# Value matmuls of two attention units issued back to back, with three buffers of probabilities

## The reference

```python
mod = (_silu(L0_c) @ L0_wmod).reshape(L0_c.shape[0], 6, 1, -1)
sa, ca, ga, sb, cb, gb = (mod[:, 0], ..., mod[:, 5])      # ga, gb kept at least 0.25 from zero
h = _layernorm(x) * (1 + ca) + sa
x = x + ga * attention(h)      # 16 heads of 16 features, causal; q, k, v, o projections with LoRA
h = _layernorm(x) * (1 + cb) + sb
x = x + gb * ffn(h)            # 1024 hidden features, relu, top 2 of 4 experts by a softmax router
```

## Time and profile before

| | |
|---|---|
| time, median of 3 runs | 1972.65 us (1972.18 to 1976.28) |
| the profiled execution: time, span | 1980.25 us, 1978.5 us |
| mean granted TensorE clock | 0.973 |
| busy share of the span | PE 91%, DVE 62%, ACT 48%, POOL 27% |
| mean DMA rate | 65 GB/s |
| one `pv` step group (L911), all units | 332.0 us busy, 3072 instructions |

### The profile page before, as it was taken

The page is one execution under the profiler, slowest core; times in us unless marked ns, Lnnn a source line. Parts: engine busy times, 40 slices in busy tenths (PEclk is TensorE's granted clock), DMA queues, the critical chain, the costliest instruction groups (busy, mean ns, idle before and its releaser), DMA issues.

```text
span 1978.5 us, 31549 instructions
## 1 busy us (share of the span) xinstructions
PE 1802.2 (91%) x10868; PEld 942.1 (48%) x10868; DVE 1234.0 (62%) x2681; ACT 941.8 (48%) x1701; POOL 532.9 (27%) x833
## 2 busy tenths in 40 slices
PE   7698889999989999999989999899999999899868
PEld 5343344454544555454644545444554545344535
DVE  3676577657676567756686577766677555753131
ACT  2255465544555455544455445544455444544320
POOL 2112122322313222233223222133222232133223
PEclk9789899999999999999999999999999999899979
DMA  7613432313321313223323223213222222220000
GB/s 179 146 54 91 82 82 55 76 42 75 74 80 39 94 44 81 68 41 76 85 60 71 52 67 85 67 41 92 60 47 66 45 76 57 39 42 23 25 0 22
DMA packets 249862, 128.69 MB, mean 65 GB/s; under 512 B 158214, under 2 KB 244834, under 8 KB 249708
## 3 DMA queue, kind: packets, MB, share of 16 engines
q1 hardware_dynamic: 245564, 125.61, 26.4%
q10 hardware_dynamic: 4144, 1.07, 0.4%
HBM read 83.06 MB, written 41.97 MB: 63 GB/s over the span
## 4 chain that ended last, share of the span: by engine, by line
PE 71%; DVE 17%; ACT 5%; issue 3%; SPq 2%; DMA 2%; POOL 0%; POOLq 0%; DVEq 0%; ACTq 0%
PE dense L855 11%; PE ov L911 11%; PE st L896 10%; PE mxs L880 8%; PE dense L998 6%; PE dense L936 5%; PE dense L841 5%; PE dense L849 4%; DVE negm L1311 4%; DVE negm_left L1311 3%; PE dense L861 3%; PE mxs L884 2%; PE dense L928 2%; ACT probs L1046 2%; SPq L651 2%
## 5 line engine op out<-in xcount | busy, mean ns | idle before, releaser
L1046 ACT ACTIVATE probs<-st 128x512 f32<-128x512 f32 (+1 forms) x1216 | 672.6, 576 | 717.6 <-PE st L896 715.1
L1311 DVE TENSOR_REDUCE negm<-mxs 128x1 f32<-128x384 f32 (+4 forms) x736 | 444.9, 617 | 258.0 <-PE mxs L884 255.3
L896 PE MATMUL st<-q_st,k_st 98*128 98x512 bf16 (+3 forms) x1536 | 451.8, 332 | 24.8 <-ACT probs L1046 17.4
L880 PE MATMUL mxs<-k_st,q_st 96*128 96x512 bf16 (+3 forms) x1280 | 401.3, 324 | 34.9 <-DVE negm_left L1311 20.8
L1311 DVE TENSOR_REDUCE negm_left<-mxs 128x1 f32<-128x512 f32 x512 | 343.1, 687 | 141.7 <-PE mxs L880 140.6
L911 PE MATMUL ov<-probs,v_g 128*32 128x512 f32 (+3 forms) x3072 | 332.0, 505 | 1.4 <-POOL probs L743 1.4
L855 PE MATMUL dense<-c_t,wi_t 128*128 128x512 f32 x512 | 266.3, 606 | 12.3 <-DVE second L1365 11.6
L880 PEld LDWEIGHTS mxs<-k_st,q_st 96*128 96x128 bf16 x1280 | 123.4, 98 | 269.9 <-issue 103.4
L756 POOL TENSOR_TENSOR hid<-hid,second 128x512 f32<-128x512 f32 x128 | 161.8, 1266 | 305.3 <-DVE second L1365 305.3
L896 PEld LDWEIGHTS st<-q_st,k_st 98*128 98x128 bf16 x1536 | 142.4, 99 | 169.6 <-ACT probs L1046 71.0
L740 POOL TENSOR_TENSOR fence<-fence 128x1 f32<-128x1 f32 x256 | 51.5, 201 | 621.8 <-ACT probs L1046 621.8
(11 more groups left out here) (165 smaller groups left out, 1700.8 us busy)
## 6 DMA issues: line engine op xcount, KB each, us to landing
q_st<-q_parts_scratch SPq DMA_DIRECT2D x384, 64.0 KB
k_st<-k_parts_scratch SPq DMA_DIRECT2D x384, 64.0 KB
q_parts_scratch<-q_part SPq DMA_DIRECT2D x16, 768.0 KB, 3.3
k_parts_scratch<-k_part SPq DMA_DIRECT2D x16, 768.0 KB, 5.2
xin<-in_L_attn_x SPq DMA_DIRECT2D x8, 1024.0 KB, 5.8
values_scratch<-v_rows SPq DMA_DIRECT2D x32, 256.0 KB, 2.1
v_g<-values_scratch SPq DMA_DIRECT2D x128, 64.0 KB, 3.9
x<-in_L_attn_x SPq DMA_DIRECT2D x16, 512.0 KB, 4.3
```

The source lines that it names most:

```text
L880: last = nc.tensor.matmul(mxs[:, bank_m, j * n:j * n + left], q_st[0:KS, slot, h0 + j, qt * P:(qt + 1) * P], k_st[0:KS, slot, h0 + j, k0:k ...
L896: last = nc.tensor.matmul(st[:, score_bank(ch, kt, h0), j * n:(j + 1) * n], k_st[0:KS + 2, slot, h0 + j, kt * P:(kt + 1) * P], q_st[0:KS + ...
L1046: nc.scalar.activation(probs[:, par, h0:h0 + heads, 0:n], st[:, score_bank(ch, kt, h0), 0:heads * n].rearrange("p (j q) -> p j q", q=n), A ...
L1311: nc.vector.tensor_reduce(dst[:, h0:h0 + heads], src, axis=AX.X, op=ALU.max, negate=True).then_inc(max_free, 1)
```

## The change

Nothing is computed differently. The parts are:

- The list has no `pv` at the end of an even slot; at the end of an odd slot k it has the `pv` of units k - 1 and k.
- `probs` has three buffers, and the exponential of a unit waits for the `pv` three units before it. The step counts gain a name, `unit`, for that.
- `o_sb` has one buffer. `v_rows` is no tensor of its own: it is a part of `hid` (tiles 4 and 5), and of `second` in the prologue. Before the relu of tile 4 of the first half ACT waits until the staged values have been stored. The setup's two gate temporaries move from `o_sb` to `ratio_b`.
- The load of `v_g` counts the `pv` steps by the new order (the same steps must be done as before).

```diff
+PROBS = 3
...
-        plan.append(("pv", g % 2, c, kt))
+        if k % 2:
+            plan += [("pv", g % 2, *v) for v in UNITS[k - 1:k + 1]]
         if kt == 4 * c + 3:
             plan.append(("ov", c))
...
+    if step[0] == "qk" and step[4] == 0:
+        names.append("unit")
...
-        v_rows = sb("v_rows", [P, 2, 2, D])
-        probs = sb("probs", [P, 2, HG, HB])
-        o_sb = sb("o_sb", [P, 2, HB])
+        probs = sb("probs", [P, PROBS, HG, HB])
+        o_sb = sb("o_sb", [P, HB])
...
-        gate_abs = o_sb[:, 0, :]
-        gate_sgn = o_sb[:, 1, :]
+        gate_abs = ratio_b[:, 0, :]
+        gate_sgn = ratio_b[:, 1, :]
+        v_rows = [f.rearrange("p (a t d) -> p a t d", a=2, t=2)
+                  for f in (second[:, :, :].rearrange("p a b -> p (a b)"), hid_f[:, T * D:T * D + 4 * D])]
...
-                    after(sp, pv_done, done("pv") - VG_UNIT - 1)
+                    after(sp, pv_done, done("pv") - VG_UNIT)
...
-                    par = UNITS.index((ch, kt)) % 2
+                    par = UNITS.index((ch, kt)) % PROBS
...
-                        after(act, pv_done, done("pv"))
+                        after(act, pv_done, done("unit") - PROBS + 1)
...
-                    nc.scalar.copy(o_sb[:, a[0], :], ov[:, :]).then_inc(ov_free, 1)
+                    nc.scalar.copy(o_sb[:, :], ov[:, :]).then_inc(ov_free, 1)
...
+                    if (half, ft) == (0, FT // 2):
+                        for i in range(2):
+                            after(act, v_out[i], 16 * done(f"vs{i}"))
...
-                    nc.scalar.copy(v_rows[:, a[0] % 2],
+                    nc.scalar.copy(v_rows[it >= 0][:, a[0] % 2],
```

More of the change, by code:

```diff
@@ L657, in run @@
                     rows = v_d[done("vs") // 4 % 2].rearrange("(t p) d -> p t d", p=P)
-                    sp.dma_start(rows[:, 2 * i:2 * i + 2, :], v_rows[:, i % 2]).then_inc(v_out[i % 2], 16)
+                    sp.dma_start(rows[:, 2 * i:2 * i + 2, :], v_rows[it >= 0][:, i % 2]).then_inc(v_out[i % 2], 16)
                 elif kind == "vg":
                     g = a[0]
-                    after(sp, pv_done, done("pv") - VG_UNIT - 1)
+                    after(sp, pv_done, done("pv") - VG_UNIT)
                     for i in range(2):
@@ L959, in run @@
                         pe.wait_ge(ov_free, done("ov"))
-                        last = turned(db, lambda t: o_sb[:, a[1], t * P:(t + 1) * P])
+                        last = turned(db, lambda t: o_sb[:, t * P:(t + 1) * P])
                     elif kind == "rb":
```

## The result

The changed kernel takes 2032.39 us (median of 4 runs, 2032.09 to 2035.49) against 1973.91 for the kernel before beside it (4 runs, 1972.18 to 1976.28): 1.0283 times as long, 95% interval 1.0269 to 1.0296. The forecast was 1997 with a range of 1972 to 2012. The direction was right. The size was not: +58 us in place of +25, outside the range.

The account below looks back on a forecast made before the run. PE's order of work was taken as the bound. A middle batch: 8.5 lost cover - 1.0 swallowed - 3.4 saved = +4.1 us, six +24.6; last body +1, first -1; +25 on 1972.65, put at 1997, range 1972 to 2012.

Parts of the forecast that it names:

- relu in 19 and 21: `fb` opening these slots waits for the previous slot's relu once the value step between is gone: 0.50 us each.
- `fa` in 17: `fa` of slot 17 needs all dense banks, the last freed by ACT: a new wait of 1.03 us.
- What the moved step uncovers: Prediction's part on waits that even slots' value steps had hidden: 8.5 us a middle batch.
- `nm` of slot 45: `nm` waits for the split maxima, already 0.89 us; all of 1.08 us was to be added.
- Slot 9: `nm` after the split maxima: DVE is the bound, PE waits longer here and shorter in slot 10; 0.
- The first body: Waits of slots 45 and 47 (1.7 us) against some 2.7 saved, as it waits more anyway: -1 us.
- The last body: Feed-forward waits of 4.3 us against at most 3.4 saved: +1 us.
- The pair's saving: Two adjacent value steps cost 0.29 instead of 0.46 us beyond streaming: 0.17 saved, 20 pairs, 3.4 us a batch.
- the boundary: Passage between a pair's two value steps, taken at 0.03 us like a half boundary; bounds 0 and 0.08.
- Rival 3: The boundary between a pair's value steps costs an entry, 0.08 instead of 0.03 us: 2005 to 2011; chance 0.12.
- Rivals 1 and 2: 1: faster, new waits replace old, 1949, chance 0.13; 2: no change, about 5 us swallowed, 1969 to 1977, chance 0.08.
- took off 1.0: Deduction per middle batch for waits in slots 45, 47, 1 and 11 (3.5 us) that may shorten existing ones.

Follow-up runs that it names:

- e1: The changed kernel with one value step at the end of every slot again, the new buffers kept; 1976.08 us, ratio to the kernel before 0.9997.
- e7: Against e1, the `nm` of slot 45 moved ahead of the value step that ends slot 44, no pairs; 1991.04 us, ratio 1.0075.
- e2: The changed kernel with single value steps in slots 8, 9, 20, 21, 32, 33, 44 and 45; 2011.05 us, ratio 1.0165.
- e8: The changed kernel with `nm` at the end of slots 9, 21, 33 and 45 instead of the start; 2000.28 us, ratio 1.0128.
- e4: The changed kernel with `fb`, where it opens an odd slot ahead of the next tile's `fa`, moved behind that `fa`; 2017.47 us, ratio 1.02.
- e5: The changed kernel with single value steps in the first body, pairs in all others; 2015.68 us, ratio 1.0193.
- e6: The changed kernel with pairs at twelve chosen places, none in the first body, and `fb` behind `fa` in slots 19, 35, 39; 1966.85 us, ratio 0.9955.

## Why the prediction was wrong in size, point by point

- **The mechanism** was right: a value step between the step that starts the other engine and the step that needs it had hidden the wait. In the middle bodies PE's idle time grew by 43.5 us, about what the prediction's waits come to there, and `e1` leaves no part of the time to the buffers, which the prediction had at nothing.
- **The single waits** came out close, as lost cover per body (the pair of slots' difference plus 0.24) against the forecast: relu in 19 and 21 0.47 and 0.67 (forecast 0.50 each), 25 0.29 (0.50), 35 and 39 0.67 and 0.64 (0.66 each), `fa` in 17 1.08 (1.03), `nm` in 33 0.55 (0.54), 27 0.67 (0.66), 47 0.59 (0.66), slot 1 1.35 (1.08), of which 0.27 is a stretch at half clock in one body of six. DVE's backlog in 40 to 43 swallowed what was to be swallowed: +0.43 and -0.64.
- **The step that failed first** is in "What the moved step uncovers", at `nm` of slot 45: "all of 1.08 is added". The wait did grow by 1.0, but the slots by 2.5, since the clock fell behind it. The prediction priced every wait by its own length, at full speed. Nine more stretches at half clock are 15 us over the middle bodies; `e7` shows the cause and the price with no pairing at all, `e2` and `e8` show it gone when the wait is. How many of the waits are followed by one no term could have given: nine here, three in `e4`, whose `nm` waits are nearly as long. Without these 15 us the middle bodies would be at +20, 5 below the forecast.
- **Slot 9** was put at 0, as DVE is the bound there. Its wait went from 0.85 to between 1.10 and 1.87 us, and the clock fell behind four of the six. Slots 8 to 11 have 2.39 - 0.27 = 2.1 us of lost cover against 0.66. "DVE is the bound" was read as slack for PE. What came back in slots 10 to 13 is only 0.27 + 0.48, and in 14/15 another 0.86 was lost.
- **The first body** was put at -1 and is +9.6, +11.5 with its first two slots. I had counted two of its waits and taken the rest for saving. The step "as it waits more anyway" was the mistake: that it waits more means that its transfers have less cover, and each even slot's value step had been a part of it. `e5` takes pairs out of this body alone and gains 16.7 us, of which the traces leave some 12.5 to the order in this body.
- **The last body** was +4.2 against +1, and no experiment was spent on it. Its `nm` waits grew only from 1.7 to 2.1 us. Slots 26/27 have +2.11, with a stretch at half clock that `e2`, `e4` and `e8` do not have there (+0.43), but slots 8/9 have one less than before, and the body has 17 us at half clock in both. What makes up the excess stays open.
- **The pair's saving** was sized 0.17 us at 20 pairs, 3.4 a body; it is 0.24 at all 24, 5.8. The entry was taken right (0.09 against 0.08), the boundary and the second step's half boundary too dear: 0.03 assumed for each, 2 ns measured, inside the bounds. The row they were taken from, 0.46 from half to half against 0.43 of streaming, holds for the first half boundary of a stay (453 ns) only. This error went in favour of the kernel and hid a part of the others. Per body: 3.4 less 7.5 forecast; 5.8 less 11.6 measured, of which 2.6 is the clock.
- **The Trainium skill's rule** on weight loads ("TensorE: Matmul & The Clock Gate", Part 3: Packing small matmuls: an overlap only where the row groups differ) would have made the boundary 0.11 us. The trace shows no such cost for this form: four value matmuls with new weights over the same rows follow four others after 429 ns with 427 ns of streaming. The prediction left out that the same part of the skill's page also lets a load into the background weight buffer go ahead of running matmuls; by that the loads would be hidden, as they are here. No run tells whether this is the reason. Rival 3 is ruled out either way.
- **The 27 us** beyond the forecast, by parts: middle bodies 10 (15 of clock less 5), first body 12 with its first two slots, last body 3, tail 1.
- **Rivals 1 and 2**, swallowing: what was swallowed outright, in 10 to 13, 36/37 and 42/43, is 0.27 + 0.48 + 0.18 + 0.64 = 1.6 us a body, not 5. The forecast took off 1.0, which was the right size.
- **The range** ended at 2012. Its upper end was made of the prices of waits and the boundary, both from rows at full clock, so no term of it could reach 2032. (The upper end of the forecast's own range, 2009, is also added up wrong: its terms give 2007 to 2008.) The profile before did show half speed, in the first and the last body (0.91 and 0.96 in the windows above) where PE waits more. The earlier trace rows have 1.00 for the middle batch, and the prediction took that as given for a batch to which it added 8 us of waits.

What stays open. When the clock falls. In slot 45 a wait of 0.89 us never did it (0 of 30 middle bodies in five kernels) and one of 1.88 did it in 16 of 30, by kernel five, five, four, one and one of six. But 1.81 us in slot 14 did it in none of six in the changed kernel, and 1.24 us in the same slot in five of six in `e6`. In slot 9 of the changed kernel it fell behind 1.82, 1.74, 1.74 and 1.65 us and not behind 1.10 and 1.87. The runs varied the order of the steps and little else, and what decides it besides the wait was not found. The tail became 1.4 us longer with unchanged work. The eleven traces have 117.1 to 122.3 us there, in no order that goes with the edits, so this can't be told from scatter.

## What to carry to other kernels

In an in-order stream every step is also a cover: before moving one, list for each later step what it waits for and when that was started, and do it separately for the bodies that lack part of the work, as they have the least cover. Price a wait of TensorE that grows towards two microseconds at itself and, as a risk, the half-speed stretch that may follow it, where TensorE is the bound; here two such waits a batch cost 15 us beside their own length, and in another order of the same steps a third of that. An edit that gains 0.24 us at a place and costs 0.5 to 2.5 at others is to be applied place by place, and the places are read after each step anew, since a gain seen behind a wait can be that wait's time given back.

## What the runs showed of the hardware

- TensorE's granted clock fell from 2.4 to 1.2 GHz for 3.4 us after it had stood idle once for 1.88 us in an otherwise busy stretch; that stretch of work took 15.48 us in place of 13.81, 1.67 us lost. It did so in 16 of 30 bodies over five kernels; after 0.89 us at the same place in none of 30.
- A stay in the 32-column form of value matmuls costs 0.24 us beyond its streaming (0.09 to enter, 0.15 within), whether one step or two are issued in it: two steps in one stay, 0.24 in all; one score matmul between them, 0.48.
- In a pair the four groups of value matmuls, each with new weights over the same rows, start 453, 429 and 429 ns apart, where 427 ns are streaming: behind the first change of weights no time is seen for the next ones.
